# A four-layer recurrent and routed-expert kernel: two layers' indirect transfers placed under other stages, and a 63-tap filter rewritten as banded matrices

## What is computed

```python
# layer 1, attention branch, v: [B, 512, 128], four heads of 32 channels
o, _ = delta_rule_chunkwise(q, k, v, beta)            # triangular solve per chunk of 32, then a scan
short = causal_depthwise(v, fir_short_w)              # 3 taps per channel
long  = causal_depthwise(v, fir_long_w)               # 63 taps per channel
stats = mean and std of short, long, o, v per head    # feed a gate network
S = rms_norm(sum_i softmax(gate)_i * branch_i) @ Wo
# layers 1, 2 and 3, expert branch: top 2 of 8, 8 and 12 experts
G[t] = w0[t] * expert[i0[t]](xn[t]) + w1[t] * expert[i1[t]](xn[t])   # layer 3: plus a shared expert
```

## Times and profile before

| | us |
|---|---|
| median of 2 runs | 4045.52 |
| the two runs | 4024.75 and 4066.28 |
| time of the profiled execution | 4024.7 |
| its span, first to last instruction | 4022.9 |
| its mean granted TensorE clock, as a share of 2.4 GHz | 0.806 |

### The profile page before, as it was taken

How to read it: one execution, slowest core, us unless ns; L and a number is a source line. 1 busy time by engine, 2 the same in 40 slices (tenths; PEclk the granted TensorE clock), 3 DMA queues, 4 the chain that set the end, 5 groups by cost and what they waited for, 6 DMA issues and landing times. The chain is left out here.

```text
span 4022.9 us, 58683 instructions
## 1 busy us (share of the span) xinstructions
PE 2594.0 (64%) x19862; PEld 1771.9 (44%) x19862; DVE 2261.7 (56%) x5007; ACT 1362.2 (34%) x2376; POOL 820.4 (20%) x824
## 2 busy tenths in 40 slices
PE   6999913633412699038429999998525383999990
PEld 3566613421412544017324555556513263676880
DVE  5555565356464489754358888883344695112443
ACT  4444401223000100222117888883213321333330
POOL 0000002206300300032536000001446660000116
PEclk9999955856555899568759999999857695899995
DMA  4000001201022000005311000004411000000761
GB/s 155 1 1 0 1 1 57 42 1 44 0 42 43 1 0 0 4 0 172 109 34 43 1 1 1 2 1 136 139 28 35 8 0 2 16 5 5 209 187 63
DMA packets 139483, 159.97 MB, mean 40 GB/s; under 512 B 55044, under 2 KB 108808, under 8 KB 138664
## 3 DMA queue, kind: packets, MB, share of 16 engines
q1 hardware_dynamic: 118392, 114.54, 10.1%
q0 software_dynamic: 20912, 43.22, 3.5%
HBM read 111.96 MB, written 45.74 MB: 39 GB/s over the span
## 5 line engine op out<-in xcount | busy, mean ns | idle before, releaser
L2403 DVE CUSTOM_DVE_ANT_0 decayed_sd<-decayed_sc,decayed_decay 128x512 f32<-128x512 f32 x512 | 331.8, 686 | 85.9 <-PE decayed_sc L2280 85.4
L2358 ACT ACTIVATE decayed_pr<-decayed_sd,decayed_shift 128x512 f32<-128x512 f32 x512 | 338.9, 713 | 49.8 <-DVE decayed_shift L2410 49.5
L2292 PEld LDWEIGHTS decayed_tr<-all_ident,decayed_pr 128*128 128x128 f32 x2048 | 223.4, 140 | 175.4 <-ACT decayed_pr L2358 100.2
L2292 PE MATMUL decayed_tr<-all_ident,decayed_pr 128*128 128x128 f32 x2048 | 276.8, 278 | 11.1 <-ACT decayed_pt L2365 10.8
L450 PE MATMUL experts_up<-experts_xt,experts_w 128*128 128x256 f32 x1140 | 271.5, 385 | 0.0
L207 PE MATMUL norm_turned<-all_ident,norm_xn 128*128 128x128 f32 x128 | 35.7, 434 | 334.3 <-DVE norm_xn L143 334.3
L1889 PE MATMUL fir_ps<-fir_padded,fir_diag 128*128 128x512 f32 x480 | 208.7, 597 | 25.0 <-POOL fir_diag L1863 25.0
L450 PEld LDWEIGHTS experts_up<-experts_xt,experts_w 128*128 128x128 f32 x1140 | 211.0, 194 | 24.5
L427 POOL DMA_DIRECT2D rows_out<-experts_y x121 | 87.7, 725 | 645.5 <-DVE experts_y L510 453.7
L2417 DVE COPY decayed_pt<-decayed_tr 128x512 f32<-128x512 f32 x256 | 173.3, 685 | 2.6 <-PE decayed_tr L2292 2.6
L207 PEld LDWEIGHTS norm_turned<-all_ident,norm_xn 128*128 128x128 f32 x128 | 22.9, 217 | 342.4 <-DVE norm_xn L143 342.4
(11 more groups left out here) (502 smaller groups left out, 5790.6 us busy)
## 6 DMA issues: line engine op xcount, KB each, us to landing
experts_w<-in_L_experts SPq DMA_DIRECT2D x78, 384.0 KB, 3.3
experts_w<-in_L_experts SPq DMA_DIRECT2D x43, 579.0 KB, 4.0
experts_tok<-rows_in SPq DMA_DIRECT2D x121, 128.0 KB, 3.4
rows_out<-experts_y POOLq DMA_DIRECT2D x121, 128.0 KB, 3.5
rows_in<-linear_zero SPq DMA_DIRECT2D x43, 128.0 KB, 1.8
experts_w<-in_L_experts SPq DMA_DIRECT2D x8, 514.0 KB, 4.0
experts_b<-in_L_experts_b SPq DMA_DIRECT2D x43, 64.0 KB, 4.2
moe_w<-in_L_moe SPq DMA_DIRECT2D x4, 514.0 KB, 3.6
```

The costliest lines, as they stand in the source:

```text
L2292: last = pe.transpose(tr[u % TURNED][:, t * P:(t + 1) * P], pr[:, u % RING, t * P:(t + 1) * P], m.ident[:, :])
L2358: act.activation(pr[:, u % RING, :], sd[:, u % RING, :], ACT.Exp, bias=shift[:, u % RING:u % RING + 1]).then_inc(exp_ready, 1)
L2403: dve.tensor_tensor_reduce(out=sd[:, u % RING, :], in0=sc[h][:, :], in1=decay[:, qt, :], scale=1.0, scalar=-3.0e38, op0=ALU.mult, op1=ALU. ...
```

## The change

1. Layer 1's sends go from conv into the second block of solve, whose matrices get a tile of their own (`L1solved`) so that `m.T`, the rows to be sent, stays whole.
2. experts1 is called between scan and fir. The 64 gathers of layer 1 are issued by GpSimd in stats, into `m.T` and a new tile; mix1 only weighs and adds.
3. Layer 3's sends are spread: six DMAs (three tiles) per block in project3, and two per block in rotate, at whose end GpSimd waits for all of them. experts3 is called straight after out3, and its gathers are issued in moe3. mix2 keeps its own gathers.
4. `fir_phase` is new. `constants_phase` writes the taps into a DRAM table of 129 rows of 384 floats, zero around the 63 taps, with one row that holds a single 1. Reading row c with a shift of one float per partition gives the banded 128x128 matrix of channel c and 64 more columns for the step into the next tile, with time in reverse order; 16 DMAs fetch them, 8 channels each, through a ring of 6. TensorE transposes v to time on the partitions (32 transposes), multiplies each channel's band with its 32 tiles of time (128 matmuls with 32 columns), adds the carry from the tile before (128 matmuls with 64 rows, 64 outputs and 24 columns), and turns the result back to heads by 32 matmuls with 512 columns with a reversing matrix. VectorE makes the short filter over the whole 4096 columns in three instructions.

The pair of rows L1908 and L1915 comes eight times, then L1925 with 32 matmuls. The diff, cut to its core (what fir_phase loses is printed above):

```diff
+def gather_rows(pool, m, rows, collected):
+
+    for n in range(NB):
+        for t in range(n * TPB, (n + 1) * TPB):
+            for k in range(2):
+                pool.indirect_dma_start(rows[k][:, t, :], None, m.rows_out, bass.IndirectOffsetOnAxis(m.SLOT[:, k, t:t + 1], 0)).then_inc(collected[n], 16)
...
         @block.gpsimd
         def _(pool):
-            for n in range(NB):
-                for t in range(n * TPB, (n + 1) * TPB):
-                    for k in range(2):
-                        pool.indirect_dma_start(rows[:, k, t, :], None, m.rows_out, bass.IndirectOffsetOnAxis(m.SLOT[:, k, t:t + 1], 0)).then_inc(collected[n], 16)
+            if gather:
+                gather_rows(pool, m, rows, collected)
...
+def constants_phase(nc, phase, m, pairs, long_taps):
...
             for to, of in pairs:
                 sp.dma_start(to, of).then_inc(loaded, 16)
+            sp.wait_ge(taps_cleared, 2)
+            sp.dma_start(taps[:, BAND - P - LONG:BAND - P], long_taps).then_inc(taps_loaded, 16)
+            sp.dma_start(m.bands[P:P + 1, :], unit[:, :]).then_inc(taps_stored, 16)
+            sp.wait_ge(taps_loaded, 16)
+            sp.dma_start(m.bands[0:P, :], taps[:, :]).then_inc(taps_stored, 16)
+            sp.wait_ge(taps_stored, 32)
             sp.wait_ge(loaded, 16 * len(pairs))
...
         @block.gpsimd
         def _(pool):
-            for t in range(NT):
-                send_tile(pool, m, t, sent)
-            pool.wait_ge(sent, 2 * NT * 16)
+            if send is not None:
+                send(pool)
...
+
+        @block.gpsimd
+        def _(pool):
+            if send is not None:
+                send(pool)
...
+BAND = 3 * P
+
+
+def fir_phase(nc, phase, m, d, v, vt, y, acc, fs, fl):
+
+    SHORT = 3
+    WIDE = 192
+    GROUP, RING = 8, 6
+    GROUPS = P // GROUP
...
+        band = s.sb("band", [P, RING, GROUP, WIDE])
...
         @block.sync
         def _(sp):
-            sp.dma_start(wl[:, :], d["L1_fir_long"]).then_inc(loaded, 16)
             sp.dma_start(ws[:, :], d["L1_fir_short"]).then_inc(loaded, 16)
...
+            sp.dma_start(flip[:, :], bass.AP(m.bands.tensor, P * BAND, [[1, P], [1, P]])).then_inc(loaded, 16)
+            for g in range(GROUPS):
+                r = g % RING
+                if g >= RING:
+                    sp.wait_ge(ps_ready, (g - RING) // 2 + 1)
+                sp.dma_start(band[:, r, :, :], bass.AP(m.bands.tensor, g * GROUP * BAND + 64, [[1, P], [BAND, GROUP], [1, WIDE]])).then_inc(band_loaded[r], 16)
...
+        @block.tensor
+        def _(pe):
+            for n in range(NB):
+                if n >= 2:
+                    pe.wait_ge(act_vt if n % 2 == 0 else dve_vt, n // 2)
...
+                    at = (n * TPB + t) * P
+                    last = pe.transpose(turned[n % 2][:, t * P:(t + 1) * P], v[:, at:at + P], m.ident[:, :])
...
+            pe.wait_ge(act_vt, NB // 2)
+            pe.wait_ge(dve_vt, NB // 2)
+            seen = [0] * RING
+            for x in range(BANKS):
+                if x >= 2:
+                    pe.wait_ge(act_y if x % 2 == 0 else dve_y, x // 2)
+                for g in range(2 * x, 2 * x + 2):
+                    seen[g % RING] += 1
+                    pe.wait_ge(band_loaded[g % RING], 16 * seen[g % RING])
+                    for c in range(g * GROUP, (g + 1) * GROUP):
+                        at = c % PER_BANK * NT
+                        pe.matmul(ps[x % 2][:, at:at + NT], band[:, g % RING, c % GROUP, 64:WIDE], by_tile(vt)[:, c, :],
+                                  start=(c % PER_BANK == 0), stop=False, skip_group_check=True)
+                for g in range(2 * x, 2 * x + 2):
+                    for c in range(g * GROUP, (g + 1) * GROUP):
+                        at = c % PER_BANK * NT
+                        later = ps[x % 2][64:P, at:at + NT].rearrange("p (b t) -> p b t", t=TPB)[:, :, 1:]
+                        sooner = by_tile(vt)[64:P, c, :].rearrange("p (b t) -> p b t", t=TPB)[:, :, 0:TPB - 1]
+                        last = pe.matmul(later, band[64:P, g % RING, c % GROUP, 0:64], sooner, start=False, stop=True, skip_group_check=True)
+                last.then_inc(ps_ready, 1)
+            pe.wait_ge(act_y, BANKS // 2)
+            pe.wait_ge(dve_y, BANKS // 2)
+            for half in range(2):
+                for j in range(4):
+                    if half == 1:
+                        pe.wait_ge(act_out if j < 2 else dve_out, j % 2 + 1)
+                    for h in range(HEADS):
+                        c = h * HD + half * PER_BANK
+                        last = pe.matmul(spread[32 * h:32 * h + 32, j, :], flip[:, 32 * j:32 * j + 32], y[:, c * NT:c * NT + 512], start=True, stop=True)
+                    last.then_inc(spread_ps, 1)
 
...
+            for n in range(0, NB, 2):
+                act.wait_ge(turned_ps, n + 1)
+                act.activation(by_tile(vt)[:, :, n * TPB:(n + 1) * TPB].rearrange("p c t -> p t c"),
+                               turned[n % 2][:, :].rearrange("p (t c) -> p t c", c=P), ACT.Copy).then_inc(act_vt, 1)
+            for x in range(0, BANKS, 2):
+                act.wait_ge(ps_ready, x + 1)
+                act.activation(y[:, x * 512:(x + 1) * 512], ps[x % 2][:, :], ACT.Copy).then_inc(act_y, 1)
+            for half in range(2):
+                for j in range(2):
+                    act.wait_ge(spread_ps, half * 4 + j + 1)
+                    to, of = result(j, half)
...
+            for n in range(1, NB, 2):
+                dve.wait_ge(turned_ps, n + 1)
+                dve.tensor_copy(by_tile(vt)[:, :, n * TPB:(n + 1) * TPB].rearrange("p c t -> p t c"),
+                                turned[n % 2][:, :].rearrange("p (t c) -> p t c", c=P)).then_inc(dve_vt, 1)
+
+            def keep_y(x):
+                dve.wait_ge(ps_ready, x + 1)
+                dve.tensor_copy(y[:, x * 512:(x + 1) * 512], ps[x % 2][:, :]).then_inc(dve_y, 1)
+
...
+            link(dve.tensor_scalar(acc[:, :], v[:, :], ws[:, SHORT - 1:SHORT], None, ALU.mult))
+            keep_y(1)
+            for lag in (1, 2):
+                kept = time(acc)[:, :, lag:]
+                link(dve.scalar_tensor_tensor(out=kept, in0=time(v)[:, :, 0:SEQ - lag], scalar=ws[:, SHORT - 1 - lag:SHORT - lag], in1=kept,
+                                              op0=ALU.mult, op1=ALU.add))
+                keep_y(1 + 2 * lag)
+            link(dve.transpose(fs[:, :], acc[:, :]))
+            keep_y(7)
+            for half in range(2):
+                for j in range(2, 4):
+                    dve.wait_ge(spread_ps, half * 4 + j + 1)
+                    to, of = result(j, half)
+                    dve.tensor_copy(to, of).then_inc(dve_out, 1)
```

```diff
+        squared = centred
+
+        @block.gpsimd
+        def _(pool):
+            gather(pool)
...
-                for t in range(n * TPB, (n + 1) * TPB):
+                for t in range(n * 3, n * 3 + 3):
                     send_tile(pool, m, t, sent)
-            pool.wait_ge(sent, 2 * NT * 16)
...
-            with pool.Fori(0, NB) as n:
+            for n in range(NB):
 
                 pool.wait_ge(r_ready, n + 1)
                 pool.tensor_tensor(half[2][:, :, :, :], side(n, 0), spread(sin), ALU.mult)
                 pool.tensor_tensor(half[3][:, :, :, :], side(n, 1), spread(cos), ALU.mult).then_inc(mult, 1)
+                send_tile(pool, m, 3 * NB + n, sent)
+            pool.wait_ge(sent, 2 * NT * 16)
...
-            fir_phase(nc, "fir", m, d, vc, b[2], (b[0], b[5]), b[1], b[3])
+            q, k, kc, vc = b[0], b[1], b[3], b[4]
+            with Scope(nc, "L1solved") as inner:
+                solved = inner.sb("solved", [P, NT * P])
+                solve_phase(nc, "solve", m, k, beta, b[5], solved, send1(0, NT))
+                delta_scan_phase(nc, "scan", m, q, k, kc, vc, solved, beta, flat_s)
+            routed_phase(nc, "experts1", m, 8, 2, "glu", d["L1_experts"], act_fn=ACT.Silu, sent=sent1)
+            fir_phase(nc, "fir", m, d, b[2], b[0], b[5], m.T[:, :, :].rearrange("p t d -> p (t d)"), b[1], b[3])
+            rows1 = (m.T, a.sb("rows", [P, NT, P]))
             branches = (b[1], b[3], flat_s, vc)
-            branch_stats_phase(nc, "stats", m, branches, b[5], b[6], b[0], b[2])
+            branch_stats_phase(nc, "stats", m, branches, b[5], b[0], b[2], lambda pool: gather_rows(pool, m, rows1, collected1))
             gate_mlp_phase(nc, "gatemlp", m, d, b[2], b[0], b[5])
-            mix_branches_phase(nc, "branches", m, d, b[5], branches, (b[6], b[2]), b[0])
+            mix_branches_phase(nc, "branches", m, d, b[5], branches, (m.XNT, b[2]), b[0])
             project_phase(nc, "out1", m, b[0], d["L1_wo"], m.S)
-            routed_phase(nc, "experts1", m, 8, 2, "glu", d["L1_experts"], act_fn=ACT.Silu, sent=sent1)
-        with Scope(nc, "L1c") as a:
-            collect_mix_phase(nc, "mix1", m, a.sb("rows", [P, 2, NT, P]))
+            collect_mix_phase(nc, "mix1", m, rows1, collected1)
...
```

(14 more changed lines are left out.)

144 lines of the change are left out of this document (48 added, 96 removed).

## The result

The changed kernel took 3724.5 us in the median of 2 runs (3723.0 to 3726.0), the kernel before 4045.5: a ratio of 0.921, 95% interval 0.900 to 0.941. The forecast was 3715 (3682 to 3775). The total held, and that it held so closely is luck: two terms of its sum missed by 44 us, and smaller errors of the other sign, one of them in a stage that nobody touched, took 28 of that back.

What follows compares the result with a forecast made beforehand. No single engine bounds the kernel: each fenced-off stage is bound by the engine that ends it, and gains add. From 4024.7 us the stage terms summed to 3709.9; a quarter of the run shift made it 3715, range 3682 to 3775.

Steps and rivals of the forecast that it cites:

- conv and solve: Layer 1's sends moved from conv to solve: conv -28.3 us, solve +1 us (0 to 4).
- At conv's pace: In solve: 64 sends at conv's 1.07 us plus 0.3 each need 88 us, covered with 49 us to spare.
- mix1, mix3: Gathers leave both stages, VectorE's part at 0.72 us per instruction remains: mix1 -58.5 us, mix3 -54 us.
- +10.5: Stats: GpSimd's 64 gathers and drain end the stage at 89 to 92 us against 80.5; range +8 to +14.
- I go by the row: Stats: conv's row (1.07 us a send against 0.99) taken over the contention rule, so stats would hardly suffer.
- a rival in which VectorE is slowed: Stats: GpSimd's descriptor writing slows VectorE, four adds cost 28 us more, stage ends at 110, total 3730; chance 0.05.
- -175: Fir: the new long filter takes 70 us instead of 245.0, summed along TensorE's path.
- At 2.4 GHz half: Fir's band products: solve's 0.43 us per matmul at 1.2 GHz halves to 0.214, so 27.4 us for 128.
- my own mark: Fir: the main step counts as wrong if the stage is over 100 or under 50 us.
- The rival's loop: Fir at half clock: loop 86 us, turn back 17, fir 118, total 3760; chance 0.2, shared with the transfer-bound case.
- The bands' transfer: Fir: 12.6 MB at about 314 GB/s take 40 us, or 47 us with unaligned pieces, hidden under TensorE's 47 us loop.
- project3, rotate: Layer 3's sends spread: project3 -21 us (-25 to -12), rotate +6 us from two sends per block, landing and drain.

## Why the prediction was right or wrong

- **What bounds the kernel**: right. The gains of fenced-off stages added up, as the run with the old filter shows.
- **conv and solve** (-28.3, +1): right, -30.9 and +1.2. The sends lay under solve with VectorE's wait for its fetch at 11.7 us instead of 11.3. "At conv's pace" was wrong there too, 1.35 us a send for 1.07, and 49 us of spare time hid it.
- **mix1, mix3** (-58.5, -54): right in mechanism, 4 us short each. The 0.72 us per instruction was too much: mix1's 40 take 26.3 us, 0.66 each, and start and end cost 1.2, not 2.7.
- **stats** (+10.5): the stage, the engine and the drain were right, the size was wrong by half: +21.6. The failed step is "I go by the row", the price of a send beside VectorE taken from conv. There the two-input instructions are of 512 elements and 0.75 us; in stats they are of 4096 and 4.4 us, and each keeps one fetch waiting for its whole length. The Trainium skill, GPSIMD Engine Reference, section 1 (Specifications), has the rule that GpSimd's SBUF interfaces contend with VectorE when that has two SBUF inputs or runs in a 2-port perf mode. The trace agrees for two inputs (5.08 us beside a subtraction, 0.94 beside a one-input reduction), and the scaling that held a fetch for 2.94 us with one input, at twice the pace, fits the second half, though no run shows its mode. I had weighed that rule in the wrong direction, as a rival in which VectorE is slowed; its subtractions kept their 4.42 us, and GpSimd paid.
- **experts1, moe3** (0, hidden): right. The window of moe3 is 285.3 us long after 286.8 before, experts1 125.1 after 126.0.
- **fir** (-175): the step that failed is "At 2.4 GHz half", in what it took for granted: the clock. By my own mark (over 100) the main step was wrong. Transposes 8.9 of the 11 with their copies, turn back 9.3 for 8.5, transfer hidden, a carry at about half a product (0.23 for 0.42): right. The loop took 83 us and not 47. The halving itself was right: the run with wide matmuls shows 0.11 us for an instruction of a product and 0.06 for one of a carry where the clock is 1.00, against 0.107 and 0.06 in the sum, which makes the 44 us estimated above. So all 36 us are the granted clock, 0.50 in all of the loop but its first two to three us, and none is the price of the instructions. The rival's loop, 86 us, was right, and I had given it 0.2; its turn back at half clock, 17, was not, since the clock came back within it. The row that I took the price from had said it: in the kernel before, L1660 ran at 0.50 with TensorE busy every microsecond, in this window of its middle:

```profile
1069.00:1090.00 21.00, 21.00 (x101) 21.00 (x100) 2.08 (x3) 0.00 (x0) 13.51 (x3) 0.50 0.00 0
```

  I read that stage's clock as that of a stage with pauses, and halved its price because "the clock was high where it was dense". Same shape, dense, and 1.2 GHz was the evidence on the spot; the old fir streams 512 columns a load, the experts 128 and more.
- **The bands' transfer**: 314 GB/s had been worked out for full engines; the loop's first window shows 328 at a share of 1.09. The 47 us that were estimated from the Trainium skill, DMA: Bandwidth & Descriptors, "How a descriptor splits into AXI transactions", are not seen: 12.6 MB at 328 GB/s are 38 us. The estimate had a slip as well. By the page's account a piece of 768 bytes with these shifts takes 24 to 32 beats, and 28 is about the mean, not the most; the 47 us are worked out from that mean. No run fetched the same pieces aligned, so what the shift costs is open.
- **project3, rotate** (-21, +6): -23.4 and +0.7. The sends fitted into GpSimd's pauses in rotate; VectorE's 44.2 of 47.1 us is what ends it.
- **The total**: +44 us in two terms, -28 in the others, of which 8.3 is causal3's. The forecast's 3715 is 9.5 us from 3724.5 by that luck, not by a sum that was right in its parts.

## What to carry to other kernels

Take the clock along with the price: when an operation's duration is read from a row, read the granted clock of that window and how busy the engine was, and halve it only if a row of the same shape shows the higher clock. If loads of weights fill TensorE, exchange the operands so that the small one is loaded and put four 32-column groups next to each other. GpSimd's indirect DMAs hide under VectorE only between instructions with two input tiles (and a long scaling of one held one too): cut long ones, and count again what a cover costs once the stage above it has become short. A price that a row gives beside short instructions is not the price beside long ones of the same kind.

## What the runs showed that I had not expected

- The granted clock fell from 1.00 to 0.50 inside a gapless stream of matmuls (products of 32 columns with 128x128 weights, PE and PEld full), stayed there with 64 columns, and rose to 1.00 again and again with 512-column matmuls in between.
- The changed kernel's loop moved 427 pieces of 768 bytes a us, the run with smaller pieces 426 of 512 bytes.
- A product with 64 columns cost what one with 32 did (55.0 and 54.2 us for 128).
- 512-column matmuls on 32-column weights cost 0.145 us an instruction with four heads in turn and 0.626 with one head, both in the mean over stretches at either clock.
- Cutting four 4.42 us subtractions into pieces of 0.70 cost VectorE 2.3 us and gave GpSimd 15.
- One untouched stage (causal3) took 140 to 150 us from kernel to kernel, with the same code of its own, and 140.8 and 141.1 in two profiles of one kernel.
